# First layer, groups 2 to 4: the conditioning product as sixteen 32x32 products on rotated strips, then transposes with a rotated identity

## The reference

```python
# first layer, conditioning: one 32x32 matrix per sample, made from 8 kernels
h = gelu(embedding @ W0 + b0); h = gelu(h @ W1 + b1)
att = softmax(h @ W2 + b2)                       # 64 x 8
agg_w = einsum('bk,koi->boi', att, weight)       # 64 x 32 x 32
agg_b = att @ bias_k
c = einsum('boi,bih->boh', agg_w, x) + agg_b[:, :, None]
# first layer, feed-forward: 512 -> 1792 -> 512
gate, up = c @ W_gate.T, c @ W_up.T
x = x + (silu(gate) * up) @ W_down.T
```

## Time and profile before

| | us |
|---|---|
| median of 3 executions | 541.61 |
| lowest and highest of them | 540.4, 541.81 |
| the profiled execution, its own time | 540.37 |
| the profiled execution, span from first to last instruction | 538.6 |

### The profile page before, as it was taken

How to read it: one execution, slowest core, us unless ns; L and a number is a source line. 1 busy time by engine, 2 the same in 40 slices (tenths; PEclk the granted TensorE clock), 3 DMA queues, 4 the chain that set the end, 5 groups by cost and what they waited for, 6 DMA issues and landing times.

```text
span 538.6 us, 6963 instructions
## 1 busy us (share of the span) xinstructions
PE 526.7 (98%) x2643; PEld 391.7 (73%) x2643; DVE 235.9 (44%) x535; ACT 141.9 (26%) x249; POOL 153.8 (29%) x153
## 2 busy tenths in 40 slices
PE   7999999999999999999999999999999999889997
PEld 6888888888888888888888886635354554567885
DVE  3522343622223623233522434544525257887665
ACT  5422222322222322222222222000002217645333
POOL 3399994400000400000300930040001100127556
PEclk9999999999999999999999999999999999999999
DMA  8398440294000230000305000959695919589863
GB/s 299 109 422 317 164 103 0 78 145 108 0 0 0 86 89 0 0 0 0 94 6 136 2 1 0 149 129 154 204 188 180 232 24 220 114 167 186 196 138 138
DMA packets 82502, 61.60 MB, mean 114 GB/s; under 512 B 61744, under 2 KB 66864, under 8 KB 81712
## 3 DMA queue, kind: packets, MB, share of 16 engines
q1 hardware_dynamic: 77696, 41.83, 35.2%
q0 software_dynamic: 4704, 19.40, 14.3%
q10 hardware_dynamic: 80, 0.08, 0.0%
HBM read 38.98 MB, written 12.81 MB: 96 GB/s over the span
## 4 chain that ended last, share of the span: by engine, by line
PE 96%; DVE 1%; ACT 1%; DMA 0%; issue 0%; POOL 0%; DVEq 0%; POOLq 0%
PE ps L684 94%; PE ps L884 1%; DMA pack_a<-in_pack_a 0%; DVE cT L1387 0%; ACT c_hi L1080 0%; PE ps L999 0%; PE ps L845 0%; PE ps L900 0%; DVE m L1400 0%; ACT cS L1148 0%; POOL silu L579 0%; ACT wT L1080 0%; PE ps L906 0%; DVE lg L1213 0%; ACT ex L1131 0%
## 5 line engine op out<-in xcount | busy, mean ns | idle before, releaser
L684 PE MATMUL ps<-c_hi,wl 128*128 128x512 f32 x448 | 169.9, 389 | 0.0
L684 PE MATMUL ps<-c_lo,wl 128*128 128x512 f32 x448 | 169.7, 389 | 0.0
L1213 DVE TENSOR_TENSOR hff<-silu,ps 128x512 f32<-128x512 f32 x56 | 38.5, 688 | 164.2 <-PE ps L684 164.2
L684 PEld LDWEIGHTS ps<-c_lo,wl 128*128 128x128 f32 x448 | 84.1, 188 | 17.5
L684 PEld LDWEIGHTS ps<-c_hi,wl 128*128 128x128 f32 x448 | 84.0, 188 | 17.4
L684 PE MATMUL ps<-wl,h_hi 128*128 128x512 f32 x224 | 87.6, 391 | 0.0
L684 PE MATMUL ps<-wl,h_lo 128*128 128x512 f32 x224 | 87.2, 389 | 0.0
L1114 ACT ACTIVATE silu<-ps 128x512 f32<-128x512 f32 x56 | 33.5, 598 | 118.6 <-PE ps L684 118.6
L1213 DVE TENSOR_TENSOR h_lo<-hff,h_hi 128x512 fp32r<-128x512 f32 x56 | 47.3, 844 | 39.1 <-ACT h_hi L1080 39.1
L1080 ACT ACTIVATE h_hi<-hff 128x512 fp32r<-128x512 f32 x56 | 35.4, 632 | 108.8 <-DVE hff L1213 108.8
L684 PE MATMUL ps<-wbase,cT 128*128 128x512 f32 x128 | 56.5, 594 | 0.0
(11 more groups left out here) (185 smaller groups left out, 565.8 us busy)
## 6 DMA issues: line engine op xcount, KB each, us to landing
wl<-in_wl POOLq DMA_DIRECT2D x14, 768.0 KB, 8.4
stg<-y_dram SPq DMA_DIRECT2D x64, 128.0 KB, 5.1
xs<-in_x SPq DMA_DIRECT2D x4, 1024.0 KB, 7.9
x_all<-in_x SPq DMA_DIRECT2D x1, 4096.0 KB, 13.8
y_dram<-prod SPq DMA_DIRECT2D x16, 256.0 KB, 2.3
x_dram<-x_all SPq DMA_DIRECT2D x4, 1024.0 KB, 6.9
x_all<-cS POOLq DMA_DIRECT2D x4, 1024.0 KB, 7.6
x_all<-in_bias POOLq DMA_DIRECT2D x4, 1024.0 KB, 11.0
```

What stands on the lines that cost most here:

```text
L684: return pe.matmul(o, l, r, start=start, stop=stop)
L1213: return dve.tensor_tensor(o, a, b, op)
```

## The change

The block-diagonal products for groups 2 to 4 are replaced by two steps. First, `mix_first` makes sixteen products of 32x32x512 directly from the 32x32 matrices: tile j, sample b goes from row strip b to column strip (b + j) mod 4 of bank 4 + j. ScalarE (tiles 0, 1) and VectorE (tiles 2, 3) copy the four banks back to `xs`. Second, `turn_first` makes sixteen 128x128 transposes of `xs`, whose identity operand is a window at column 32 j of a doubled identity (128x224), so that the strips land in their order again, in banks 4 to 7 by chunk, as before. The last two `down` calls of the group are cut in parts that stand between these steps. GpSimd copies the 32x32 matrices to `blk` instead of building the block diagonal, and makes the doubled identity once.

```diff
+WIDE = 2 * P - ROWS
+        ident_wide = sb("ident_wide", [P, WIDE])
+        ACT_ROWS, DVE_ROWS = (0, 1), (2, 3)
@@ gpsimd
+            def weights_of(g):
+                pool.wait_ge(s_cond_mm[0], g * S)
+                pool.tensor_copy(blk[:, :, 0:ROWS], agg[:, 0, g * GT:(g + 1) * GT]).then_inc(s_blk[0], 1)
+
+            pool.tensor_copy(ident_wide[:, 0:P], ident).then_inc(s_wide, 1)
+            pool.tensor_copy(ident_wide[:, P:WIDE], ident[:, 0:WIDE - P]).then_inc(s_wide, 1)
             for g in range(1, G):
-                block_diagonal(0, g)
+                weights_of(g)
                 split_c(g)
@@ tensor
-            def down(g, m):
+            def down(g, m, js=range(GT)):
                 pe.wait_ge(s_h_lo, g * M + m + 1)
                 w = wl0[:, m, 2 * S * P:2 * S * P + D]
-                for j in range(GT):
+                for j in js:
+            def ready_to_mix(g):
+                pe.wait_ge(s_staged[0], 16 * (g + 1))
+                pe.wait_ge(s_blk[0], g + 1)
+                pe.wait_ge(s_h, g * M)
+
+            def mix_first(g):
+                for j in range(GT):
+                    for b in range(TB):
+                        at, to = slice(b * ROWS, (b + 1) * ROWS), (b + j) % TB
+                        ins = mm(bank(4 + j)[to * ROWS:(to + 1) * ROWS], blk[at, j, 0:ROWS], xs[at, j])
+                ins.then_inc(s_mixed0, 1)
+
+            def turn_first(g):
+                pe.wait_ge(s_wide, 2)
+                pe.wait_ge(s_rows0_act, len(ACT_ROWS) * g)
+                pe.wait_ge(s_rows0_dve, len(DVE_ROWS) * g)
+                for s in range(S):
+                    for j in range(GT):
+                        ins = pe.transpose(bank(4 + s)[:, cols(j)], xs[:, j, cols(s)],
+                                           ident_wide[:, j * ROWS:j * ROWS + P])
+                    ins.then_inc(s_cond_mm[0], 1)
             def layer0(g, more):
                 for m in range(M):
                     gate_up(g, m)
-                    if m >= 1 and (more or m < M - 1):
+                    if 1 <= m < M - 1:
                         down(g, m - 1)
-                pe.wait_ge(s_h, g * M + M - 1)
                 if more:
-                    cond(0, g + 1, UPPER, [nothing, nothing, lambda: pe.wait_ge(s_h, g * M + M), nothing])
+                    down(g, M - 2, (0, 1, 2))
+                    ready_to_mix(g + 1)
+                    down(g, M - 2, (3,))
+                    mix_first(g + 1)
+                    down(g, M - 1, (0, 1, 2))
+                    turn_first(g + 1)
+                    down(g, M - 1, (3,))
                 else:
+                    pe.wait_ge(s_h, g * M + M - 1)
...
-                down(g, M - 1)
+                    down(g, M - 1)
@@ scalar, after the 14 slices
                 if more:
+                    act.wait_ge(s_mixed0, g + 1)
+                    for j in ACT_ROWS:
+                        copy(xs[:, j], bank(4 + j)).then_inc(s_rows0_act, 1)
                     split_c(g + 1)
@@ vector, after the 14 slices
                 if more:
+                    dve.wait_ge(s_mixed0, g + 1)
+                    for j in DVE_ROWS:
+                        dve.tensor_copy(xs[:, j], bank(4 + j)).then_inc(s_rows0_dve, 1)
                     cond(0, g + 1, UPPER)
                     split_c(g + 1)
```

More of the change, by code:

```diff
@@ L255, in build @@
         s_blk = [sem(f"s_blk{i}") for i in range(4)]
+        s_wide = sem("s_wide")
+        s_mixed0 = sem("s_mixed0")
+        s_rows0_act = sem("s_rows0_act")
+        s_rows0_dve = sem("s_rows0_dve")
         s_cond_mm = [sem(f"s_cond_mm{i}") for i in range(4)]
@@ L717, in _ @@
             mm(bank(0), ones[:], terms).then_inc(s_bias0, 1)
-            def nothing():
-                pass
             def cond_chunk(l, g, s, b):
```

## The result

The changed kernel takes 550.07 us (median of 5 runs, 549.45 to 550.54); the kernel before takes 541.15 (5 runs, 540.4 to 541.81). The ratio is 1.016, 95% interval 1.0149 to 1.0172: 8.9 us slower, where 0.8 us less than the median of before had been forecast. The profiled execution has a span of 547.6 us against 538.6.

A forecast was written before the change was run, and what follows sets the result against it. TensorE alone was taken to bound the kernel; 0.5 us saved less 0.25 stall a place, three times, 0.8 us, gave 539.6 from the profiled 540.37, or 540.8 us as a median. Range: 538.9 to 543.2 us.

The forecast's parts named there:

- part 7: GpSimd's matrix and identity copies, the xs load, queued stores and TensorE's loop jump: all taken as costing nothing.
- Part 1: Sixteen mixing products at each changed place: start 0.1 us after the old conditioning's start, last 1.07 us, bounds 1.0 to 1.3.
- t0: Start of the old conditioning at a changed place, 252.66 us in the profile of the kernel before.
- The first rival: In mix_first, four row strips into one bank take turns: 2.9 us more a place, 549.5 us in all; chance 6%.
- Part 2: Six down records of slice 13 after the mixing: 0.31 us plus 5 x 0.226, together 1.44, without waiting.
- Part 3: Copies back to xs: start 1.12 us after the mixing starts, last 1.29, just hidden behind down records; cost 0.
- Part 4: Sixteen transposes take 1.75 us, window into the wider identity free; with tile 3 of down 13, 0.5 us less a place.
- Part 5: Slice 0 of the next group waits for late c_hi chunks: 0.25 us lost a place, bounds 0 and 0.8.
- T: Forecast start of the transposes at a changed place, t0 + 2.6 us.
- Part 6: VectorE's later adds to x_all delay slice 0's hff by 0.9 us, hidden by 0.65: cost 0, upper bound 0.4.
- The sum: Over the three changed places: 0.5 - 0.25 = 0.25 us less each, 0.8 us in all; bounds -0.6 to +0.8 a place.
- the third rival: At the changed places the trade is even: the stall takes the whole 0.5 us, giving 541.6 us; chance 20%.

The follow-up runs named there:

- experiment 1: Kernel before plus one unused 128x224 fp32 tile (896 bytes a partition) where the doubled identity stands, no instruction changed: 549.55 us against 541.04, ratio 1.0151.
- experiment 2: Changed kernel with 32 more unused columns in the doubled identity, so tiles behind it move by 1024 bytes, not 896: 541.57 us against 541.04, ratio 1.0007.
- h2_signals: Changed kernel, doubled identity at 1024 bytes, one signal after each tile's four products instead of one after the sixteenth: 541.62 us against 541.4, ratio 1.0006.
- h1_spread: Changed kernel, doubled identity at 1024 bytes, a signal after each tile's four products, down parts spread in another order: 541.63 us against 541.4, ratio 1.0003.
- i1_swap: h1_spread with the copies exchanged, VectorE taking tiles 0 and 1, ScalarE tiles 2 and 3: 540.69 us against 541.72 for the kernel before, ratio 0.9984.

## Why the prediction was wrong, point by point

- **What bounds it**: right, TensorE alone in one chain. But the sum took the pace of 0.226 us as a property of the instruction. It is one of the instruction and of where its operands lie, and the path holds 1344 of them. The step that failed is part 7, "at no cost": it counted the two copies that fill the doubled identity and not the 896 bytes that it takes. The pad alone costs 8.5 us (experiment 1), and the change with the weights level takes 541.57 us (experiment 2), so all but some 0.5 of the 8.9 us is the displacement.
- **Part 1, mixing**: M = t0 + 0.1 and 1.07 us, as forecast. The first rival (the banks take turns) is refuted, though its 549.5 us is nearly the time measured: the number fell near by chance, and the timeline shows the step at its cheap price. The Trainium skill ("TensorEngine Tiling (Array Packing)", Restrictions and Gotchas) says that different row tiles can't access the same PSUM bank at the same time. This run differs: four row strips wrote each bank, in different quarters of the partitions, and the sixteen products took the same 1.07 us as with one strip a bank in layer 2. What strips in the same quarter of a bank do, no run shows.
- **Part 2, down 13, tiles 0 to 2**: 0.34 and 5 x 0.23 for 0.31 and 5 x 0.226, right within 0.1.
- **Part 3, the copies**: mis-sized. The reader's start was taken from layer 2, where the signal that it waits for is that of the first bank. Here it comes with the last product, 1.32 instead of 1.12, and the copies cost 0.19 where 0 was taken. A signal for each tile alone does not help, because tile 2 is ready only at 1.31 (`h2_signals`, `h1_spread`); the assignment of the tiles has to change as well (`i1_swap`).
- **Part 4, transposes**: 100.36 - 98.67 = 1.69 us for 1.75. The window into the wider identity costs nothing.
- **Part 5, slice 0**: with the weights level 0.35 us of stall for 0.25, within the bounds; in the changed kernel the eight high records take 2.14 us, from 100.93 to the first low record at 103.07. The low part of chunk 3 is asked for at T + 5.0 and not T + 4.8, which changes nothing.
- **Part 6, VectorE's backlog**: hidden; in the changed kernel slice 0's down starts at 108.67, 0.23 after the record ahead of it (108.44), so it does not wait.
- **The sum**: with the weights level a place costs 5.10 + 0.35 = 5.45 us against 5.40, not 5.15. Without the displacement the time would have been 541.6, within the range; the third rival (an even trade) describes it. The 550.07 us measured lie outside the range because the range held no term for rows that the change does not touch.

## What to carry to other kernels

A new tile moves every tile declared behind it. On a path of back-to-back matmuls, write down where the two operands lie before and after the edit, and keep their distance a multiple of 256 bytes: here the other distances tried (32, 64 and 128 bytes, modulo 256) cost 6 to 7 ns on each fp32r matmul of the first layer, 1.4 to 1.7% of the kernel. When a forecast slowdown appears at the forecast size, look at the row that should carry it before believing the mechanism; here the rival had the right number and the wrong place.

## What was not expected of the hardware

- The start distance of 128x512 fp32r matmuls in the first layer depends on the distance of the operands' addresses modulo 256 bytes: 0.2265 us when level, 0.233 on average at 32, 64 and 128 bytes. How it divides within a pair differs: 0.237 and 0.229 at 128 bytes (experiment 1), 0.233 and 0.233 at 64. Moving both by 128 bytes made no difference. One displaced operand in a pair lengthens both starts of the pair.
- Two other kinds of product show little or nothing of it. `cT` and `wbase`, the operands of the fp32 products of the second layer, stood 128 apart modulo 256 in the kernel before and stand level in the changed one, with a mean of 594 ns in both. `sgn`, the weights of the last layer, moved from level to 128 apart, and the means of its 120 fp32r records grew by 1 to 4 ns (`c_hi` 424 to 426, `c_lo_odd` 396 to 400), against 3 to 10 ns in the first layer. Why they pay less is not shown.
- Of sixteen 32x32 products issued in a row, the first bank's were read from 1.12 us after the start and the third bank's from 1.31 (`h1_spread`); a single signal behind the last costs the readers of the first banks 0.2 us.
